# A graph network and two mixtures of experts on one Trainium2 core: 49 blocks of nodes in place of 50

## What is computed

```python
x = x + _L0_gnn_ref(_layernorm(x), edge_attr_8, Wq, Wk, Wv, Wo, src, dst)
x = x + _L0_ffn_ref(_layernorm(x)[None], W1, b1, Wg, bg, Wd, bd)[0]
x = x + _L1_gnn_ref(_layernorm(x), W, attn_src, attn_dst, edge_index, edge_type_8)
x = x + _L1_ffn_ref(_layernorm(x)[None], router_w, w1, b1, w2, b2)[0]
```

## Time and profile before

| | |
|---|---|
| median of three runs | 4670.19 us (4669.13 to 4671.12) |
| the profiled execution | 4661.37 us |
| its span, first to last instruction | 4659.5 us |
| mean granted TensorE clock | 0.921 |
| TensorE matmuls, busy | 4005.9 us, 86% |
| VectorE, busy | 3083.2 us, 66% |
| GpSimd, busy | 2281.4 us, 49% |
| ScalarE, busy | 2013.7 us, 43% |
| HBM traffic over the span | 128 GB/s |

### The profile page before, as it was taken

The page is one execution under the profiler, slowest core; times in us unless marked ns, Lnnn a source line. Parts: engine busy times, 40 slices in busy tenths (PEclk is TensorE's granted clock), DMA queues, the critical chain, the costliest instruction groups (busy, mean ns, idle before and its releaser), DMA issues. The chain is left out here.

```text
span 4659.5 us, 77523 instructions
## 1 busy us (share of the span) xinstructions
PE 4005.9 (86%) x21539; PEld 3198.9 (69%) x21540; DVE 3083.2 (66%) x8660; ACT 2013.7 (43%) x5648; POOL 2281.4 (49%) x2410
## 2 busy tenths in 40 slices
PE   8788888888888997999899777777777768999999
PEld 4566666666667996999544456655665647888888
DVE  5599999999995552111222278888888776666665
ACT  2455555555542332333233465656565532222222
POOL 5477777777762452000222277777777741111111
PEclk9999999999998998999899878788787789999999
DMA  6577777777763111111344555555555530000000
GB/s 214 184 205 203 207 204 205 206 204 202 205 172 136 40 39 49 37 36 35 117 183 174 196 173 158 170 165 161 168 160 167 155 116 30 16 16 17 17 16 12
DMA packets 233288, 602.19 MB, mean 129 GB/s; under 512 B 47156, under 2 KB 120024, under 8 KB 217128
## 3 DMA queue, kind: packets, MB, share of 16 engines
q0 software_dynamic: 119504, 368.96, 28.2%
q1 hardware_dynamic: 113496, 229.82, 14.0%
HBM read 494.26 MB, written 104.35 MB: 128 GB/s over the span
## 5 line engine op out<-in xcount | busy, mean ns | idle before, releaser
L274 POOL DMA_INDIRECT attn_KV<-kv_tab,attn_stage x880 | 930.9, 1058 | 280.1 <-issue 248.3
L1832 POOL DMA_INDIRECT rel_V<-h_tab,rel_stage x880 | 881.5, 1002 | 309.0 <-issue 238.8
L1935 PE MATMUL rel_SP<-rel_V,rel_OH 128*128 128x264 f32 x1760 | 608.3, 486 | 1.8 <-DVE node L2002 1.3
L387 PE MATMUL attn_SP<-attn_KV 128*128 128x264 f32 x1760 | 491.1, 404 | 25.5 <-DVE node L489 25.2
L375 PE MATMUL attn_QP<-node,attn_OHT 128*128 x1760 | 502.0, 410 | 10.8 <-issue 5.1
L2211 ACT ACTIVATE moe_HT<-moe_HB,moe_b 128x128 f32<-128x128 f32 x800 | 228.1, 368 | 565.4 <-PE moe_HB L2227 565.4
L1935 PEld LDWEIGHTS rel_SP<-rel_V,rel_OH 128*128 128x128 f32 x1760 | 382.1, 238 | 75.1 <-ACT rel_OH L1870 7.6
L387 PEld LDWEIGHTS attn_SP<-attn_KV 128*128 128x128 f32 x1760 | 341.5, 199 | 98.4 <-issue 42.2
L2227 PE MATMUL moe_HB<-moe_YT,moe_W 128*128 128x128 f32 x3200 | 401.8, 279 | 0.0
L2002 DVE TENSOR_TENSOR node<-node,rel_SP 128x264 f32 x880 | 366.3, 416 | 52.1 <-PE rel_SP L1935 31.5
L2227 PEld LDWEIGHTS moe_HB<-moe_YT,moe_W 128*128 128x128 f32 x3200 | 379.9, 193 | 19.3 <-issue 16.6
(11 more groups left out here) (343 smaller groups left out, 6894.7 us busy)
## 6 DMA issues: line engine op xcount, KB each, us to landing
rel_OHT<-dst_rows SPq DMA_DIRECT2D x55, 1024.0 KB, 6.1
h_tab<-pr_H SPq DMA_DIRECT2D x50, 1056.0 KB, 4.0
attn_KV<-kv_tab,attn_stage POOLq DMA_INDIRECT x880, 3.7
rel_V<-h_tab,rel_stage POOLq DMA_INDIRECT x880
kv_tab<-qkv_KV SPq DMA_DIRECT2D x50, 256.0 KB, 2.1
attn_runs<-runs SPq DMA_DIRECT2D x55, 192.0 KB
rel_runs<-runs SPq DMA_DIRECT2D x55, 192.0 KB
Wd<-in_wd SPq DMA_DIRECT2D x8, 1024.0 KB
```

Of the source, the lines that this page charges most:

```text
L274: pool.indirect_dma_start(out=KV[:, i * IT + u, 0:2 * FEAT], out_offset=None, in_=d["kv_tab"][:, :], in_offset=bass.IndirectOffsetOnAxis(a ...
L387: mm = pe.matmul(SP[v % SUMS][:, 0:NUMC], KV[:, j * IT + u, 0:P], KV[:, j * IT + u, FEAT:ROW], start=(u % 2 == 0), stop=(u % 2 == 1))
L1832: pool.indirect_dma_start(out=V[:, i * IT + u, :], out_offset=None, in_=d["h_tab"][:, :], in_offset=bass.IndirectOffsetOnAxis(ap=stage[:, ...
L1935: pe.matmul(SP[(c * IT + u) % SUMS][:, 0:NUMC], OH[:, j * IT + u, :], V[:, j * IT + u, :], start=True, stop=True).then_inc(s["sums"], 1)
```

## The change

`BLOCKS` is computed from the number of nodes, which gives 49. Everything that is derived from it follows: `NPAD` is 6272, `SORTED` is 56, the tables in HBM, `m.node` and the loops by blocks are smaller by one block. The gate's counting by pairs then has a last pair of one block, 48: its tiles are cut to the width `w`, the columns of `hot` for the missing block are cleared, and `LAG` becomes 4, so that turn 52, which places block 48, still exists.

```diff
-BLOCKS = 50
+BLOCKS = -(-N // P)
@@ attend_and_route
-        LAG = 3
+        LAG = 3 + BLOCKS % 2
@@ share(t, k)
-                    ex = two(m.ex[:, n * EXPERTS:(n + 2) * EXPERTS])
-                    prob = m.prob[:, n:n + 2]
+                    w = min(2, BLOCKS - n)
+                    ex = two(m.ex[:, n * EXPERTS:(n + w) * EXPERTS])
+                    prob = m.prob[:, n:n + w]
...
+                    picked, chosen = two(pick[:, 0:w * EXPERTS]), two(hot[:, 0:w * EXPERTS])
                     at = n // 2 * 8 + 2 * k
                     if k == 0:
-                        dve.wait_ge(s["powed"], n + 2)
-                        dve.tensor_reduce(inv[:, :], ex, AX.X, ALU.add).then_inc(s["share"], 1)
+                        dve.wait_ge(s["powed"], n + w)
+                        dve.tensor_reduce(inv[:, 0:w], ex, AX.X, ALU.add).then_inc(s["share"], 1)
...
                     if k == 3:
                         dve.wait_ge(s["share"], at)
-                        dve.tensor_reduce(top[:, :], two(pick[:, :]), AX.X, ALU.min).then_inc(s["share"], 1)
+                        dve.tensor_reduce(top[:, 0:w], picked, AX.X, ALU.min).then_inc(s["share"], 1)
                         dve.wait_ge(s["share"], at + 1)
-                        dve.tensor_tensor(two(hot[:, :]), each, wide(top[:, :]), ALU.is_equal).then_inc(s["share"], 1)
+                        if w == 1:
+                            dve.memset(hot[:, EXPERTS:], 0.0)
+                        dve.tensor_tensor(chosen, each, wide(top[:, 0:w]), ALU.is_equal).then_inc(s["share"], 1)
@@ place(t, k), k == 2
-                        dve.tensor_reduce(spot_of[:, n:n + 2], two(spot[:, :]), AX.X, ALU.add).then_inc(s["place"], 1)
+                        w = min(2, BLOCKS - n)
+                        dve.tensor_reduce(spot_of[:, n:n + w], two(spot[:, 0:w * EXPERTS]), AX.X, ALU.add).then_inc(s["place"], 1)
                         dve.wait_ge(s["place"], at + 1)
-                        dve.tensor_copy(m.slot[:, n:n + 2], spot_of[:, n:n + 2]).then_inc(s["slotted"], 1)
+                        dve.tensor_copy(m.slot[:, n:n + w], spot_of[:, n:n + w]).then_inc(s["slotted"], 1)
@@ tables()
-                    dve.wait_ge(s["place"], BLOCKS // 2 * 6)
+                    dve.wait_ge(s["place"], -(-BLOCKS // 2) * 6)
```

More of the change, by code:

```diff
@@ L1281, in share @@
                         return
-                    ex = two(m.ex[:, n * EXPERTS:(n + 2) * EXPERTS])
-                    prob = m.prob[:, n:n + 2]
-                    wide = lambda a: a.unsqueeze(2).to_broadcast([P, 2, EXPERTS])
-                    each = numbers[:, :].unsqueeze(1).to_broadcast([P, 2, EXPERTS])
+                    w = min(2, BLOCKS - n)
+                    ex = two(m.ex[:, n * EXPERTS:(n + w) * EXPERTS])
+                    prob = m.prob[:, n:n + w]
+                    wide = lambda a: a.unsqueeze(2).to_broadcast([P, w, EXPERTS])
+                    each = numbers[:, :].unsqueeze(1).to_broadcast([P, w, EXPERTS])
+                    picked, chosen = two(pick[:, 0:w * EXPERTS]), two(hot[:, 0:w * EXPERTS])
                     at = n // 2 * 8 + 2 * k
                     if k == 0:
-                        dve.wait_ge(s["powed"], n + 2)
-                        dve.tensor_reduce(inv[:, :], ex, AX.X, ALU.add).then_inc(s["share"], 1)
+                        dve.wait_ge(s["powed"], n + w)
+                        dve.tensor_reduce(inv[:, 0:w], ex, AX.X, ALU.add).then_inc(s["share"], 1)
                         dve.wait_ge(s["share"], at + 1)
-                        dve.reciprocal(inv[:, :], inv[:, :]).then_inc(s["share"], 1)
+                        dve.reciprocal(inv[:, 0:w], inv[:, 0:w]).then_inc(s["share"], 1)
                     if k == 1:
                         dve.wait_ge(s["share"], at)
-                        dve.tensor_tensor(ex, ex, wide(inv[:, :]), ALU.mult).then_inc(s["share"], 1)
+                        dve.tensor_tensor(ex, ex, wide(inv[:, 0:w]), ALU.mult).then_inc(s["share"], 1)
                         dve.wait_ge(s["share"], at + 1)
@@ L1299, in share @@
                         need(dve, s["counted"], n // 2)
-                        dve.tensor_tensor(two(hot[:, :]), ex, wide(prob), ALU.is_equal).then_inc(s["share"], 1)
+                        dve.tensor_tensor(chosen, ex, wide(prob), ALU.is_equal).then_inc(s["share"], 1)
                         dve.wait_ge(s["share"], at + 1)
-                        dve.tensor_tensor(two(pick[:, :]), two(hot[:, :]), each, ALU.mult).then_inc(s["share"], 1)
+                        dve.tensor_tensor(picked, chosen, each, ALU.mult).then_inc(s["share"], 1)
                     if k == 3:
                         dve.wait_ge(s["share"], at)
-                        dve.tensor_reduce(top[:, :], two(pick[:, :]), AX.X, ALU.min).then_inc(s["share"], 1)
+                        dve.tensor_reduce(top[:, 0:w], picked, AX.X, ALU.min).then_inc(s["share"], 1)
                         dve.wait_ge(s["share"], at + 1)
-                        dve.tensor_tensor(two(hot[:, :]), each, wide(top[:, :]), ALU.is_equal).then_inc(s["share"], 1)
+                        if w == 1:
+                            dve.memset(hot[:, EXPERTS:], 0.0)
+                        dve.tensor_tensor(chosen, each, wide(top[:, 0:w]), ALU.is_equal).then_inc(s["share"], 1)
                 def place(t, k):
```

## The result

The changed kernel takes 4619.07 us (median of four runs, 4615.99 to 4620.01); the kernel before, run beside it, 4670.65 us (4669.13 to 4674.16). The ratio is 0.9887, with a 95% interval of 0.987 to 0.9904: faster by 52.8 us, 44.8 to 60.7. The predicted 4622.9 us is 3.8 us above, inside its range of 4613 to 4633.

What follows compares the result with a forecast made beforehand. TensorE matmuls were taken to bound the stages by blocks, GpSimd's gathers and VectorE the edge stages. Turns of 2.80 + 0.22 + 6.61 + 14.5 + 7.53 + 15.66 = 47.3 us off 4670.19 gave 4622.9 us, range 4613 to 4633.

Steps and rivals of the forecast that it cites:

- Stage 1: Projections: one turn less between copies of keys and values, -2.80 us; 0 if the tables set the end.
- Stage 3: Gate: one turn without a counting goes, -6.61 us; GpSimd's tail keeps its length and moves with the last exponential.
- Stage 4: Sorted tiles: two tiles fewer at 7.25 us each, -14.5 us.
- Stage 5: Relations: one written-out turn less, -7.53 us.
- rival A: Stage starts fall otherwise against the clock: up to 16.5 us on or off 4622.9, likely about 8; chance 0.10.
- The bound of 16.5 us: Clock at the starts of stages 4, 5 and 7: at most half of 33.0 us of slow TensorE work, either way.
- Stage 7: Top two: one written-out turn less between last additions, -15.66 us.
- Stages 2 and 6: Edge stages paced by gathers: only clearings shrink, -0.22 and 0 us; moving over 5 us would be wrong.
- rival C: Moved HBM tables slow the 1760 gathers; another 56 ns each would give 4721.5 us; chance 0.04.
- B: Something other than the blocks sets the ends of stages 1 and 3: 9.4 us stay, 4632.3 us; chance 0.06.
- D: SORTED stays at 58 in stage 4, so 14.5 us stay: 4637.4 us; chance 0.02.
- The spread: Whole kernel: three runs of the same kernel lie within 2 us, cited against large clock effects.

Runs made afterwards that it cites:

- the other chip: The changed kernel, unedited, run again on a chip where the kernel before takes 5029.65 us: 4973.59 us, ratio 0.9906 to the kernel before.
- The 51 blocks: The changed kernel's code with BLOCKS set to 51, run twice against the kernel before: 4742.59 us (ratio 1.0149) and 4748.37 us (1.0147).
- the tiles alone: The kernel before, still 50 blocks, with SORTED set to 56 in place of 58 and nothing else: 4656.48 us, ratio 0.996.
- the old places: The changed kernel with its HBM tables allotted the rows of 50 blocks, only the first 49 used: 4625.36 us, ratio 0.9897 to the kernel before.

## Why the prediction was right, point by point

- **The sum** of 47.3 us stands against 52.8 (44.8 to 60.7) and, on the other chip, 47.3 (36.7 to 57.8). The stages by blocks alone, at equal clock or repeated, gave 7.0 + 14.3 + 8.7 + 16.5 = 46.5 where the forecast had 44.3 for them. Stage 1 adds a few: 178.8 to 184.8 us in seven profiled executions with 50 blocks (mean 181.2), 176.0 to 180.7 in five with 49 (mean 177.8), so some 3.4 of which 2.80 were forecast; its own scatter is as large.
- **Stage 3:** the mechanism held (tail unchanged, zeros moved with the exponential, the fourth lag free; of the added clearing the tail shows nothing). Its size was mis-chosen by 0.4 us: TensorE gained 7.06 us, the turn with a counting, and not the 6.61 taken. Both kernels have 25 countings, but as the two orders of TensorE ahead of the prediction show, three now stand behind the last hidden features where two did, so that one less stands ahead of them. The 51 blocks bear this out. There are 26 countings there, and again three of them stand behind, so as many stand ahead as with 50 blocks. From block 40 to the last hidden features it is 64.67 us in place of 58.04, 6.63 more, a turn without a counting.
- **Stage 4:** 14.5 forecast, 14.1 to 14.7 measured, by the tiles alone as well.
- **Stage 5:** 7.53 forecast, 8.7 measured. The turn is right to the hundredth; what the sum lacked is 0.2 us at the start and rival A in its small form, a low clock some 2 us shorter there, which was worth 1.0 us. The bound of 16.5 us was far too wide: it has all the slow work of three starts change its clock, and in this stage only matmuls around the rise did. The Trainium skill ("TensorE: Matmul & The Clock Gate", Part 1) says that the number of slow matmuls at a start varies from run to run. The traces agree for stage 3 (2.4 us between two executions of the kernel before) and for stage 5 with 51 blocks (9.84 and 8.30 us between its first two blocks), but not for stage 5 of the kernel before and of the changed one (9.74 and 9.73, 8.79 and 8.70), nor for stage 7, whose length stays within 0.5 us (825.7 to 826.2) in the profiled runs of 50 blocks.
- **Stage 7:** 15.66 forecast, 16.3 to 16.7 measured: the turn, 0.3 us in and around the loop, and 0.4 at the start (0.7 on the other chip).
- **Stages 2 and 6:** forecast at -0.22 and 0, and neither to move by over 5 us. Both clearings lost their 0.22 us. But these stages differ by more than that between executions of one kernel: stage 6 took 1183.4 to 1193.7 us with 50 blocks on one group of chips, and 1347.9 with 49 on the other chip. That an edge stage moved by 5 us was therefore badly chosen as a sign of rival C. The shortest and the median gather of stage 6 (940 to 942 and 946 ns in every run but those of 51 blocks) are a steadier one, and they did not move.
- **Rivals:** B falls. Stage 3 gave its turn whole, and in stage 1 the first instruction of the next stage follows the last copy of keys and values by 3.9 to 4.0 us in all fourteen traces, so the blocks set its end. C falls for this change, by the old places tried with the new blocks, but its price is real: with 51 blocks the gathers of stage 6 take some 50 ns more on average, for a cause that stays open. D falls by the x2800 matmuls of stage 4.
- **The spread** was put too low. Three runs within 2 us were taken as the kernel's own scatter; fifteen lie 23 us apart. The range held since the median of several runs moves far less. It does not follow from its own terms, either: 9.4 us of rival B and 8 of the clock together reach 4640, and 4633 has room for one of them only. The 4619.07 us lie 3.8 below the forecast; the stages account for some 2 of these (0.4 in stage 3, 1.2 in stage 5, 0.6 in stage 7), and the rest is within the scatter of runs, so that part is luck.

## What to carry to other kernels

Where barriers cut a kernel into stages, a saving can be worked out stage by stage from the distance between equal instructions of consecutive blocks, and it arrives whole wherever the last engine's tail hangs on the last block and not on a count of its own. Before a stage's length is held against another's, look at the same stage in two executions of one kernel, and at the clock in its first microseconds: here two executions of one kernel differed by 3 us in the gate, most of it the clock's, and by 10 us in a stage by edges, with no edit between them. A size that is rounded up costs its full turn in every stage, and a loop over a pair of turns may cost half a microsecond more than the same turns written out.

## What had not been expected of the hardware

- With 51 blocks the gathers of stage 6 take 1049 and 1056 ns on average (shortest 952) in two profiled executions, in place of 1002 to 1015 (shortest 942) with 49 or 50 blocks on such chips; unused rows and columns of that size do not bring it about.
- One chip ran the two stages by edges of the changed kernel 192 and 161 us longer than another (5029.65 against 4670 us for the whole kernel before), with gathers as long as elsewhere but more idle time before each: 472.9 us in place of 309.0 in stage 6, while no stage by blocks differed by more than a microsecond at equal clock.

```profile
L1837 POOL DMA_INDIRECT rel_V<-h_tab,rel_stage x880 | 869.8, 988 | 472.9 <-issue 239.4 <-DMA gate_X<-in_x 116.9 <-PE rel_SP L1940 59.8
```

- The low clock after the barrier ahead of stage 5 lasted 32.3 to 33.0 us in seven executions with 50 blocks, and 29.9 to 33.7 us in five with 49: a stretch that one set of kernels repeats closely need not carry over to the next.
